# Softmax row sums taken from the value matmuls, through two columns of ones behind each head's values

## The chip, the cores and the metric

The kernel runs on one core of one Trainium2 chip. The number compared is device time in microseconds for one launch, a median over runs. The core has five engines with queues of their own: TensorE (PE in the profile, with its weight loads as PEld), VectorE (DVE), ScalarE (ACT), GpSimd (POOL) and SyncE (SP, which only issues DMAs here). They wait for one another through semaphores alone.

## The reference, cut to what matters

The input `x` is (8, 512, 128). It is normalised, a small chunked attention gives `s`, and a six-layer local-attention transformer gives `g`; the output is `x + s * silu(...)`. The change lies in the attention of the six layers (16 heads of 64, windows of 32 positions, each looking at itself and the window before):

```python
def attn_layer(x, Wqkv, qs, ksc, Wo):
    q, k, v = jnp.split(x @ Wqkv, 3, -1)          # each (b, 512, 1024), 16 heads of 64
    q, k = rotary(l2norm(q) * qs), rotary(l2norm(k) * ksc)
    bk2, bv2 = look(k), look(v)                   # the window before and the window itself
    sim = einsum('bhwie,bhwje->bhwij', q, bk2) * 8, masked
    attn = softmax(sim, -1)                       # over 64 keys
    return einsum('bhwij,bhwje->bhwie', attn, bv2) @ Wo
...
for i in range(6):
    x = attn_layer(shift_tokens(x), ...) + x
    x = ffn_layer(shift_tokens(x), ...) + x       # layer norm, W1, gelu gate, W2
```

The kernel divides by the softmax denominator after the product with the values, not before: `out = (exp(sim - max) @ v) / rowsum(exp(sim - max))`.

## The kernel before

After the setup and the chunked attention (the first 0.7 ms) the program runs six layers. In a layer each of the eight sequences is one **round** (`round_`), so there are 48 rounds; a last, partial one drains the pipeline. A round has eight **iterations** `i = 0..7`, one for each pair of heads, and every engine runs its own loop over `i`, written out by hand. Nothing reorders the work: the order on an engine is the order in the code, and the semaphores (`cur["ssq"]`, `cur["o"]`, ...) tie the engines together. Iteration `i` mixes stages of different pairs: projection and norms of pair `i`, scores of pair `i - 1`, values and outputs of pair `i - 3` (modulo 8, across rounds).

What stands in one iteration, by engine, in order:

- **PE**: `project(i, 0)` (q: six matmuls L782 to L784), `middle` (chunks of v, or feed-forward matmuls of the sequence), `values(i)` (L857), `project(i, 1)` (k), `turn_probs` (L832, transposes of the probabilities), `squares(i, 0)` (L798, L799: sums of squares for the norm of q), `scores` (L812 mask, L822), `turn_out` (L870), `squares(i, 1)` (the same for k), `end`.
- **DVE**: `rotary(i, 0)` (`rb` L1090 and `ra` L1092 read PSUM; `sqlo` L1094 reads two operands in SBUF), `outputs(i)` (L1120 writes `on`), `rotary(i, 1)`, `guard(i, 0)` (L1101), `row_sums(i)` (L1129 sums the rows of `pr`, L1132 takes the reciprocal), `guard(i, 1)` (L1101), `subtract_max(i)` (L1108, L1111). In iteration 4 the DVE also does `fc` (L1162) behind `outputs` and `fl` (L1168) between `guard(4, 0)` and `row_sums`; in 6 two feed-forward products `gx` (L1140) ahead of `outputs`.
- **ACT**: `square` (L960), `exp` (L993), `values_read` (L975: a chunk of v from PSUM to the tile `v`), `inverse_norm` (L966, L968), `pt` (L1014), `oT` (L1028).
- **POOL**: `normalise(i, 1)` (L1054 on `kn`), `rotate` (L1047, the additions `qn` and then `kn`), `normalise(i, 0)` (L1054 on `qn`). All read two operands in SBUF.
- **SP**: twice a round, two DMAs (L1071, L1072) that copy half of `v` shifted by one window into its second plane.

`guard(i, k)` waits for `ssq`, which `squares(i, k)` on PE signals; PE's `squares(i, 1)` in turn waits for `guard(i, 0)`, since both use the bank `SS`. `rb` of `rotary(i, k)` waits for `project(i, k)`.

The value matmuls of `values(i)`: for each of 8 windows in two row groups and 2 heads, 32 matmuls of 64 rows by 32 columns of weights (`pt`) over 64 columns of `v`. The profile counts 64 for them, two for each matmul in float32, and as many for the scores. They wait for `pt`, for the last `outputs`, in iterations 3 and 7 for the DMAs of `v`, and in iterations 4, 5, 6 their second half waits for a reader of the bank (`filled`).

Of the kernel before, what the change touches and what calls it, by code (L numbers as in the profile page):

```python
# [20 lines left out]
P = 128  # L21
# [18 lines left out]
INNER = HEADS * DH  # L40
HP = HEADS // 2
HALF = DH // 2
DI = int(D * 4 * 2 / 3)
NJ = -(-DI // P)
JW = [min(P, DI - P * j) for j in range(NJ)]
# [472 lines left out]
def transformer(nc, t, ctx, sb0, sem, clear, con, ident, ps, xT, d_raw, d_ff):  # L518
# [5 lines left out]
    def sb(name, shape, dt=F32):  # L524
# [20 lines left out]
    pairr = sb("pairr", [P, P], F32R)  # L545
    pairb = sb("pairb", [P, P], BF16)
    xhs, xls = sb("xhs", [P, 2, S], F32R), sb("xls", [P, 2, S], F32R)
    v = sb("v", [P, 2, TB, INNER])
    sq = sb("sq", [P, 2, S])
    sqlo = sb("sqlo", [P, 2, S], F32R)  # L550
    r1 = sb("r1", [P, 2, S])
# [24 lines left out]

    names = ("xh v vev ab sq sl rot g ssq r ln add qkn S m sub exp rs ri pt ptev o oev ot otev wo x1 "
             "fx mean fc fq var fe fr fn fh fl w1 gx gl h w2 x2 shifted cleared").split()  # L580
    sets = [{n: sem(f"r{k}_{n}") for n in names} for k in range(2)]
    A, BB, SS, S0, S1, TT, O0, O1 = range(8)
# [15 lines left out]
    with nc.Block(no_gpsimd_drain=True) as block:  # L598
        @block.sync
        def _(sp):  # L600
            sp.dma_start(raw[:], t["L0_ffn_Wqkv"][0]).then_inc(d_raw, 16)
            for i, n in ((0, "L0_ffn_q_scale"), (2, "L0_ffn_k_scale")):
                src = t[n].rearrange("l (d o) -> d l o", o=1)
                for g in range(4):
                    own, other = (g % 2) * HALF, (1 - g % 2) * HALF
                    sp.dma_start(svec[g * HALF:(g + 1) * HALF, :, i:i + 1], src[own:own + HALF],
                                 allow_slow_non_contiguous=True).then_inc(d_w, 16)
                    sp.dma_start(svec[g * HALF:(g + 1) * HALF, :, i + 1:i + 2],
                                 src[other:other + HALF], allow_slow_non_contiguous=True).then_inc(d_w, 16)
            sp.wait_ge(d_w, 16 * 16)  # L610

        @block.scalar
        def _(act):
            act.wait_ge(s_vz, 1)
            for i, n in ((V_G, "L0_ffn_ln_g"), (V_B, "L0_ffn_ln_b"), (V_B2, "L0_ffn_b2")):
                act.dma_start(vecs[:, :, i:i + 1], t[n].rearrange("l (d o) -> d l o", o=1),
                              allow_slow_non_contiguous=True).then_inc(d_vec, 16)
            b1 = t["L0_ffn_b1"].rearrange("l (d o) -> d l o", o=1)
            for a in range(2):
                for j in range(NJ):  # L620
                    o = a * DI + j * P
                    c = V_B1 + a * NJ + j
                    act.dma_start(vecs[0:JW[j], :, c:c + 1], b1[o:o + JW[j]],
                                  allow_slow_non_contiguous=True).then_inc(d_vec, 16)
            act.wait_ge(d_vec, 16 * (3 + 2 * NJ))

        @block.gpsimd
        def _(pool):

            zeros = (wo[:], w2[:], vec[:], v[:, 1], qn[:], kn[:], pt[:])  # L630
            for z in zeros:
                nc.gpsimd.memset(z, 0.0).then_inc(s_set, 1)
            for z in (w1h, w1l, xhs, xls):
                nc.gpsimd.memset(z[:].bitcast(F32), 0.0).then_inc(s_set, 1)
            for z in (pr, r1, stat):
                nc.gpsimd.memset(z[:], 1.0).then_inc(s_set, 1)
            pool.wait_ge(s_set, len(zeros) + 7)

        @block.vector
        def _(dve):  # L640
            nc.vector.memset(vecs[:], 0.0).then_inc(s_vz, 1)
            nc.vector.memset(v[:, 0], 0.0).then_inc(s_vz, 1)
            nc.vector.memset(oT[:], 0.0).then_inc(s_vz, 1)
            nc.vector.memset(fx[:], 0.0).then_inc(s_hi, 1)
            nc.vector.memset(gx[:], 0.0).then_inc(s_hi, 1)
            nc.vector.memset(xT[:, B, :], 0.0).then_inc(s_hi, 1)
            nc.vector.tensor_copy(maskb[:], con[:, C_MASK:C_MASK + 256]).then_inc(s_hi, 1)
            nc.vector.tensor_copy(identb[:], ident).then_inc(s_hi, 1)
            nc.vector.tensor_copy(pairr[:], con[:, C_PAIR:C_PAIR + P]).then_inc(s_hi, 1)
            nc.vector.tensor_copy(pairb[:], con[:, C_PAIR:C_PAIR + P]).then_inc(s_hi, 1)  # L650
            dve.wait_ge(s_hi, 7)
            dve.wait_ge(s_vz, 3)
# [88 lines left out]
    def round_(k, follows, half, pb, nb, drain=False):  # L741
# [6 lines left out]
        def live(i, lag):  # L748
            return full or i < lag
# [28 lines left out]
        def tensor(pe):  # L778
# [57 lines left out]
            def values(i):  # L836
# [9 lines left out]
                for whi in range(2):  # L846
# [3 lines left out]
                    for tb in range(TB):  # L850
                        for wlo in range(2):
                            for e in range(2):
                                strip = (tb % 2 * 2 + wlo) * WIN
                                c = (e * 2 + tb // 2) * P + strip
                                o = (tb // 2) * P + e * DH
                                hh = 2 * hp + e
                                last = nc.tensor.matmul(  # L857
                                    ps[strip:strip + WIN, O0 + whi, o:o + DH],
                                    pt[whi * DH:(whi + 1) * DH, (i - 1) % 2, c:c + WIN],
                                    v[whi * DH:(whi + 1) * DH, 1 - wlo, tb, hh * DH:(hh + 1) * DH],  # L860
                                    start=True, stop=True, skip_group_check=True,
                                    tile_position=(whi * DH, strip))
                last.then_inc(cur["o"], 1)
# [89 lines left out]
        def scalar(act):  # L953
# [16 lines left out]
            def values_read(j):  # L970
# [1 line left out]
                if j == 4:  # L972
                    act.wait_ge(cur["o"], 3)
                hf, tb = j // 4, j % 4
                nc.scalar.copy(v[:, 0, tb, hf * 512:(hf + 1) * 512], ps[:, V_AT[j][2], :]).then_inc(cur["vev"], 1)  # L975

            def gate(j, bank, n):

# [85 lines left out]
        def sync(sp):  # L1064

            for hf in range(2 if full else 0):
                c = slice(512 * hf, 512 * hf + 512)
                sp.wait_ge(cur["vev"], 4 * hf + 4)
                if hf:
                    sp.wait_ge(cur["o"], 3)  # L1070
# [13 lines left out]
        def vector(dve):  # L1084
# [30 lines left out]
            def outputs(i):  # L1115

                dve.wait_ge(cur["o"], i + 1)
                after(dve, "ri", i)
                after(dve, "ot", i)
                nc.vector.tensor_tensor(  # L1120
                    on[:].rearrange("p (w g d) -> p w g d", w=2, g=4),
                    ps[:, O0:O1 + 1, 0:256].rearrange("p w (g d) -> p w g d", g=4),
                    stat[:, (i - 1) % 2, 2, :].rearrange("p (w g) -> p w g", w=2).unsqueeze(3)
                    .broadcast_to([P, 2, 4, DH]), ALU.mult).then_inc(cur["oev"], 1)

            def row_sums(i):
                b = i % 2
                dve.wait_ge(cur["exp"], i + 1)
                nc.vector.tensor_reduce(stat[:, b, 1, :], pr[:, b, :].rearrange("p (g k) -> p g k", g=8),  # L1129
                                        AX_X, ALU.add).then_inc(cur["rs"], 1)  # L1130
                dve.wait_ge(cur["rs"], i + 1)
                nc.vector.reciprocal(  # L1132
                    stat[:, b, 2, :].rearrange("p (w t e) -> p e t w", w=2, t=2),
                    stat[:, b, 1, :].rearrange("p (e t w) -> p e t w", e=2, t=2)).then_inc(cur["ri"], 1)

            def gated(j, bank, n):
                m = JW[j]
# [6 lines left out]
            for i in range(HP):  # L1144
# [21 lines left out]
                if i == 4:  # L1166
                    dve.wait_ge(cur["fh"], 1)
                    nc.vector.tensor_tensor(fl[:], fc[:], fh[:].bitcast(F32), ALU.subtract).then_inc(cur["fl"], 1)  # L1168
                if live(i, 2):
                    row_sums(i)  # L1170
                if full:
                    guard(i, 1)
                if i == 6:
# [106 lines left out]
```

## Time and profile before

| | before |
|---|---|
| median of 3 runs | 5195.39 us (5191.45 to 5198.09) |
| span of the profiled execution | 5196.3 us |
| PE busy | 4059.5 us (78%) |
| DVE busy | 4157.5 us (80%) |
| ACT busy | 2852.2 us (55%) |
| POOL busy | 2552.5 us (49%) |

The span is from the first to the last instruction of one profiled execution, and it lies inside the range of the timed runs, so what is around it is too small to be seen. The busy shares are means over stages that differ: the first 0.7 ms have little PE work. A high share does not say that an engine is waited for. In the timeline each row is one instruction, or a few alike in a row (x2, x64), with its start and its length in us; what stands in brackets is how long its engine had been idle before it and who ended the wait. On DVE a row begins about 0.08 us before the one ahead of it ends when nothing holds it, so starts 0.60 apart belong to lengths of 0.68.

### The profile page before, as it was taken

What the parts mean: (1) busy time and instruction counts of PE and PEld (TensorE: products, weight loads), DVE (VectorE), ACT (ScalarE), POOL (GpSimd) and SP (SyncE); (2) the same over time, 40 slices, a digit from 0 to 9 for tenths busy, and PEclk for the clock granted to TensorE, in tenths of its full rate; (3) what the DMA queues carried; (4) which work ended last, traced back from release to release, by engine and by line L of the source; (5) the groups of instructions that cost most, each with busy time, mean ns of one, the idle gap of its engine ahead of it and who ended that gap; (6) DMA issues with size and microseconds to landing.
All of it is one profiled execution on the core that took longest, in us unless ns stands there. A gap on an engine that the chain in (4) does not pass through costs nothing. (4 is left out here: it accounts for less than half of the span.)

```text
span 5196.3 us, 147973 instructions
## 1 busy us (share of the span) xinstructions
PE 4059.5 (78%) x62298; PEld 2893.8 (56%) x63066; DVE 4157.5 (80%) x6032; ACT 2852.2 (55%) x4736; POOL 2552.5 (49%) x1604
## 2 busy tenths in 40 slices
PE   2012048999979999789999789999799997899996
PEld 2011036666656666566666566666566665666664
DVE  5977978888878888778888788888788887788885
ACT  1011036666656666556666566666566665565665
POOL 3665844544435544445455445445355444454542
PEclk8566579999989999999999999999899999999998
DMA  0000011111111111111111111111111111111112
GB/s 21 0 6 6 0 43 37 25 25 25 25 45 25 25 25 25 33 37 25 25 25 25 33 37 25 25 25 25 46 25 25 25 25 33 37 25 25 25 25 57
DMA packets 86314, 139.19 MB, mean 27 GB/s; under 512 B 14457, under 2 KB 35600, under 8 KB 83984
## 3 DMA queue, kind: packets, MB, share of 16 engines
q1 hardware_dynamic: 78698, 127.06, 9.3%
q8 instruction: 524, 8.59, 0.7%
q10 hardware_dynamic: 6950, 2.39, 0.2%
q14 instruction: 142, 1.16, 0.1%
HBM read 30.59 MB, written 4.46 MB: 7 GB/s over the span
## 5 line engine op out<-in xcount | busy, mean ns | idle before, releaser
L1054 POOL TENSOR_TENSOR kn<-kn,r 128x512 f32<-128x512 f32 x385 | 495.6, 1287 | 1659.0 <-ACT r L968 1659.0
L960 ACT ACTIVATE sq<-ps 128x512 f32<-128x512 f32 x768 | 459.3, 598 | 905.8 <-PE ps L784 901.7
L1090 DVE TENSOR_TENSOR rb<-ps,tab 128x512 f32<-128x512 f32 x768 | 527.7, 687 | 404.7 <-PE ps L784 346.1
L966 ACT ACTIVATE r<-r 128x512 f32<-128x512 f32 x769 | 485.7, 632 | 567.3 <-DVE r L1101 566.7
L1054 POOL TENSOR_TENSOR qn<-qn,r 128x512 f32<-128x512 f32 x384 | 495.4, 1290 | 550.0 <-ACT r L968 550.0
L1047 POOL TENSOR_TENSOR kn<-ra,rb 128x512 f32<-128x512 f32 x384 | 631.2, 1644 | 79.7 <-DVE ra L1092 70.2
L1094 DVE TENSOR_TENSOR sqlo<-sq 128x512 fp32r<-128x512 f32 x768 | 644.9, 840 | 0.0
L782 PE MATMUL ps<-xhs,wl 128*128 128x512 f32 x768 | 403.5, 525 | 237.3 <-PEq L122 178.5
L1101 DVE TENSOR_SCALAR r<-ps 128x512 f32<-128x512 f32 x768 | 524.2, 683 | 29.0 <-remote 10.5
L1047 POOL TENSOR_TENSOR qn<-ra,rb 128x512 f32<-128x512 f32 x384 | 537.6, 1400 | 0.0
L857 PEld LDWEIGHTS ps<-v,pt 64*32 64x32 f32 x24768 | 394.2, 108 | 243.7 <-issue 186.9
L1092 DVE TENSOR_TENSOR ra<-ps,tab 128x512 f32<-128x512 f32 x768 | 522.2, 680 | 5.7 <-ACT sq L960 5.7
L857 PE MATMUL ps<-v,pt 64*32 64x64 f32 x24768 | 472.6, 223 | 44.7 <-DVE gx L1140 34.1
L968 ACT ACTIVATE r<-r 128x512 f32<-128x512 f32 x769 | 485.5, 631 | 24.4
L798 PE MATMUL ps<-sqlo,pairr 128*128 128x512 f32 x768 | 364.3, 474 | 146.0 <-DVE r L1101 146.0
L822 PE MATMUL ps<-kn,qn 64*32 64x64 f32 x24640 | 426.2, 220 | 19.0 <-POOL kn L1054 15.9
L822 PEld LDWEIGHTS ps<-kn,qn 64*32 64x32 f32 x24640 | 364.0, 106 | 105.2 <-POOL kn L1054 70.1
L418 PE MATMUL ps<-con,ob 128*128 128x128 f32 x36 | 9.9, 431 | 521.3 <-DVE ob L510 521.3
L1120 DVE TENSOR_TENSOR on<-ps,stt 128x512 f32<-128x512 f32 x387 | 265.9, 687 | 105.3 <-PE ps L857 105.3
L913 PE MATMUL ps<-oT,wo 128*128 128x512 f32 x784 | 346.6, 595 | 3.8
L782 PEld LDWEIGHTS ps<-xhs,wl 128*128 128x128 f32 x768 | 146.7, 191 | 312.5 <-issue 244.2
L782 PE MATMUL ps<-xhs,sl 128*128 128x512 f32 x768 | 309.2, 403 | 0.0
(182 smaller groups left out, 9161.1 us busy)
## 6 DMA issues: line engine op xcount, KB each, us to landing
v<-v SPq DMA_DIRECT2D x96, 768.0 KB, 5.8
v<-v SPq DMA_DIRECT2D x96, 192.0 KB, 5.7
raw<-in_L_ffn_Wqkv SPq DMA_DIRECT2D x7, 1536.0 KB, 7.3
tab<-in_rotary SPq DMA_DIRECT2D x6, 1024.0 KB, 5.7
raw<-in_L_ffn_Wo SPq DMA_DIRECT2D x6, 512.0 KB
sT<-so ACTq DMA_DIRECT2D x3, 768.0 KB, 3.3
xnat<-in_L_attn_hidden_states SPq DMA_DIRECT2D x8, 256.0 KB, 3.4
srow<-sT SPq DMA_DIRECT2D x8, 256.0 KB, 3.1
```

The lines of the kernel that those rows point to most:

```text
L782: nc.tensor.matmul(dst, al, bh, start=True, stop=False)
L822: last = nc.tensor.matmul(ps[strip:strip + WIN, S0 + e, col:col + 2 * WIN], q[:, wd * WIN:(wd + 1) * WIN], k[:, wd * WIN:(wd + 2) * WIN], ...
L857: last = nc.tensor.matmul(ps[strip:strip + WIN, O0 + whi, o:o + DH], pt[whi * DH:(whi + 1) * DH, (i - 1) % 2, c:c + WIN], v[whi * DH:(whi ...
L960: nc.scalar.activation(sq[:, k, :], ps[:, A, :], ACT.Square).then_inc(cur["sq"], 1)
L966: nc.scalar.activation(r1[:, k, :], r1[:, k, :], ACT.Ln, scale=RN * RN).then_inc(cur["ln"], 1)
L968: nc.scalar.activation(r1[:, k, :], r1[:, k, :], ACT.Exp, scale=-0.5).then_inc(cur["r"], 1)
L1047: nc.gpsimd.tensor_tensor(dst, ra[:, k, :], rb[:, k, :], ALU.add).then_inc(cur["add"], 1)
L1054: nc.gpsimd.tensor_tensor(dst, dst, r1[:, k, :], ALU.mult).then_inc(cur["qkn"], 1)
L1090: nc.vector.tensor_tensor(rb[:, k, :], ps[:, BB, :], tab[:, 2 * k + 1, :], ALU.mult)
L1092: nc.vector.tensor_tensor(ra[:, k, :], ps[:, A, :], tab[:, 2 * k, :], ALU.mult).then_inc(cur["rot"], 1)
L1094: nc.vector.tensor_tensor(sqlo[:, k, :], sq[:, k, :], sq[:, k, :].bitcast(BF16)[:, 1::2], ALU.subtract).then_inc(cur["sl"], 1)
L1101: nc.vector.tensor_scalar(r1[:, k, :], ps[:, SS, :], 1e-24, None, ALU.max).then_inc(cur["g"], 1)
```

## The change

`v` gets 66 columns a head (`DV = DH + 2`) in place of 64; the two behind the values hold ones from the setup on, in both planes. `values` runs over 66 columns, so that columns 64 and 65 of each head's result are the row sum of the same probabilities; a head's result takes 66 columns of PSUM in place of 64. `row_sums` is gone. `outputs` waits for `o`, takes the reciprocal of column 64 of each of the eight results straight from PSUM, waits for it, and multiplies. `values_read` copies a chunk in eight pieces of 64 columns with a step of 66. The DMAs of `v` carry 528 columns a row in place of 512.

```diff
+DV = DH + 2
-    v = sb("v", [P, 2, TB, INNER])
+    v = sb("v", [P, 2, TB, HEADS * DV])
-            zeros = (wo[:], w2[:], vec[:], v[:, 1], qn[:], kn[:], pt[:])
+            zeros = (wo[:], w2[:], vec[:], qn[:], kn[:])
...
-            for z in (pr, r1, stat):
-                nc.gpsimd.memset(z[:], 1.0).then_inc(s_set, 1)
+            for z in (pr[:], r1[:], stat[:], v[:, 1], pt[:]):
+                nc.gpsimd.memset(z, 1.0).then_inc(s_set, 1)
...
-            nc.vector.memset(v[:, 0], 0.0).then_inc(s_vz, 1)
+            nc.vector.memset(v[:, 0], 1.0).then_inc(s_vz, 1)
...  values(i)
-                                o = (tb // 2) * P + e * DH
+                                o = (tb // 2 * 2 + e) * DV
                                 hh = 2 * hp + e
                                 last = nc.tensor.matmul(
-                                    ps[strip:strip + WIN, O0 + whi, o:o + DH],
+                                    ps[strip:strip + WIN, O0 + whi, o:o + DV],
                                     pt[whi * DH:(whi + 1) * DH, (i - 1) % 2, c:c + WIN],
-                                    v[whi * DH:(whi + 1) * DH, 1 - wlo, tb, hh * DH:(hh + 1) * DH],
+                                    v[whi * DH:(whi + 1) * DH, 1 - wlo, tb, hh * DV:(hh + 1) * DV],
...  values_read(j)
-                nc.scalar.copy(v[:, 0, tb, hf * 512:(hf + 1) * 512], ps[:, V_AT[j][2], :]).then_inc(cur["vev"], 1)
+                nc.scalar.copy(v[:, 0, tb, hf * 8 * DV:(hf + 1) * 8 * DV].rearrange("p (h d) -> p h d", h=8)[:, :, 0:DH],
+                               ps[:, V_AT[j][2], :].rearrange("p (h d) -> p h d", h=8)).then_inc(cur["vev"], 1)
...  sync
-                c = slice(512 * hf, 512 * hf + 512)
+                c = slice(8 * DV * hf, 8 * DV * (hf + 1))
...  outputs(i)
                 dve.wait_ge(cur["o"], i + 1)
-                after(dve, "ri", i)
+                o4 = ps[:, O0:O1 + 1, 0:4 * DV].rearrange("p w (g d) -> p w g d", g=4)
+                ri = stat[:, (i - 1) % 2, 2, :].rearrange("p (w g) -> p w g", w=2).unsqueeze(3)
+                nc.vector.reciprocal(ri, o4[:, :, :, DH:DH + 1]).then_inc(cur["ri"], 1)
+                dve.wait_ge(cur["ri"], i + 1)
                 after(dve, "ot", i)
                 nc.vector.tensor_tensor(
-                    on[:].rearrange("p (w g d) -> p w g d", w=2, g=4),
-                    ps[:, O0:O1 + 1, 0:256].rearrange("p w (g d) -> p w g d", g=4),
-                    stat[:, (i - 1) % 2, 2, :].rearrange("p (w g) -> p w g", w=2).unsqueeze(3)
+                    on[:].rearrange("p (w g d) -> p w g d", w=2, g=4), o4[:, :, :, 0:DH], ri
                     .broadcast_to([P, 2, 4, DH]), ALU.mult).then_inc(cur["oev"], 1)
-            def row_sums(i):
...
                 if i == 4:
                     dve.wait_ge(cur["fh"], 1)
                     nc.vector.tensor_tensor(fl[:], fc[:], fh[:].bitcast(F32), ALU.subtract).then_inc(cur["fl"], 1)
-                if live(i, 2):
-                    row_sums(i)
                 if full:
                     guard(i, 1)
```

Where instructions stand now, first on DVE in iteration 2, from `outputs` to `subtract_max` (`r` is the tile `r1` of the two guards, `stt` the tile of maxima, sums and reciprocals); before:

```order
L1120 TENSOR_TENSOR on<-ps,stt 128x512
L1090 TENSOR_TENSOR rb<-ps,tab 128x512
L1092 TENSOR_TENSOR ra<-ps,tab 128x512
L1094 TENSOR_TENSOR sqlo<-sq 128x512
L1101 TENSOR_SCALAR r<-ps 128x512
L1129 TENSOR_REDUCE stt<-pr 128x8
L1132 RECIPROCAL stt<-stt 128x2x2x2
L1101 TENSOR_SCALAR r<-ps 128x512
L1108 TENSOR_REDUCE stt<-ps 128x8
L1111 TENSOR_TENSOR pr<-ps,stt 128x512
```

and after:

```order
L1122 RECIPROCAL stt<-ps 128x8
L1125 TENSOR_TENSOR on<-ps,stt 128x512
L1092 TENSOR_TENSOR rb<-ps,tab 128x512
L1094 TENSOR_TENSOR ra<-ps,tab 128x512
L1096 TENSOR_TENSOR sqlo<-sq 128x512
L1103 TENSOR_SCALAR r<-ps 128x512 x2
L1110 TENSOR_REDUCE stt<-ps 128x8
L1113 TENSOR_TENSOR pr<-ps,stt 128x512
```

The sum over `pr` has gone from between the two guards, which now follow each other directly, and the reciprocal has moved up, to right ahead of `on`, where it reads PSUM.

On PE in iteration 2, from the last matmuls of `project(2, 0)` over `values(2)` to `project(2, 1)`; before:

```order
L783 MATMUL ps<-xls,sh 128x512
L784 MATMUL ps<-xhs,sh 128x512
L782 MATMUL ps<-wh,xls 128x512
L783 MATMUL ps<-wl,xhs 128x512
L784 MATMUL ps<-wh,xhs 128x512
L857 MATMUL ps<-v,pt 32x64 x32
L782 MATMUL ps<-xhs,wl 128x512
```

and after:

```order
L784 MATMUL ps<-xls,sh 128x512
L785 MATMUL ps<-xhs,sh 128x512
L783 MATMUL ps<-wh,xls 128x512
L784 MATMUL ps<-wl,xhs 128x512
L785 MATMUL ps<-wh,xhs 128x512
L858 MATMUL ps<-v,pt 32x66 x32
L783 MATMUL ps<-xhs,wl 128x512
```

Nothing moves on PE, nor on ACT, POOL (in the rounds) and SP; the 32 value matmuls of an iteration have 66 columns in place of 64.

## Rows read from the trace of the kernel before

**Rows 1.** The page, part 1: busy us, share of the span, instructions of each engine

```profile
PE 4059.5 (78%) x62298; PEld 2893.8 (56%) x63066; DVE 4157.5 (80%) x6032; ACT 2852.2 (55%) x4736; POOL 2552.5 (49%) x1604
```

**Rows 2.** Timeline (start us, us, engine line op out<-in xcount), iteration 1

```profile
2574.07 1.27 POOL L1047 TENSOR_TENSOR qn<-ra,rb 128x512 f32<-128x512 f32 x1
...
2574.52 1.36 DVE L1094 TENSOR_TENSOR sqlo<-sq 128x512 fp32r<-128x512 f32 x1
...
2575.81 0.68 DVE L1101 TENSOR_SCALAR r<-ps 128x512 f32<-128x512 f32 x1
2576.41 0.67 DVE L1129 TENSOR_REDUCE stt<-pr 128x8 f32<-128x512 f32 x1
...
2576.63 0.47 PE L798 MATMUL ps<-sqlo,pairr 128*128 128x512 f32 x1 [0.67 <-DVE r L1101]
...
2577.11 0.20 DVE L1132 RECIPROCAL stt<-stt 128x8 f32<-128x8 f32 x1
...
2577.38 0.69 DVE L1101 TENSOR_SCALAR r<-ps 128x512 f32<-128x512 f32 x1
```

**Rows 3.** Timeline of iteration 6 of the same round

```profile
2628.78 0.69 PE L857 MATMUL ps<-v,pt 64*32 64x64 f32 x32 [0.71 <-DVE gx L1140]
...
2632.37 0.68 DVE L1094 TENSOR_TENSOR sqlo<-sq 128x512 fp32r<-128x512 f32 x1
2632.39 1.79 POOL L1047 TENSOR_TENSOR qn<-ra,rb 128x512 f32<-128x512 f32 x1
...
2633.94 0.48 PE L798 MATMUL ps<-sqlo,pairr 128*128 128x512 f32 x1
...
2634.70 0.69 DVE L1101 TENSOR_SCALAR r<-ps 128x512 f32<-128x512 f32 x1 [0.21 <-remote]
```

**Rows 4.** Groups by line: x count | busy us, mean ns of one | idle before

```profile
L1101 DVE TENSOR_SCALAR r<-ps 128x512 f32<-128x512 f32 x768 | 524.2, 683 | 29.0 <-remote 10.5
...
L913 PE MATMUL ps<-oT,wo 128*128 128x512 f32 x784 | 346.6, 595 | 3.8
...
L1108 DVE TENSOR_REDUCE stt<-ps 128x8 f32<-128x512 f32 x385 | 261.6, 680 | 2.8 <-PE ps L822 2.8
L1129 DVE TENSOR_REDUCE stt<-pr 128x8 f32<-128x512 f32 x386 | 259.1, 671 | 0.0
...
L1028 ACT COPY oT<-ps 128x512 f32<-128x512 f32 x387 | 219.8, 568 | 7.9 <-PE ps L870 7.9
L975 ACT COPY v<-ps 128x512 f32<-128x512 f32 x384 | 217.3, 580 | 24.0 <-PE ps L784 23.9
...
L1132 DVE RECIPROCAL stt<-stt 128x8 f32<-128x8 f32 x386 | 79.3, 205 | 13.2
```

**Rows 5.** Timeline of iteration 4, into the start of iteration 5

```profile
2612.19 1.16 DVE L1168 TENSOR_TENSOR fl<-fc,fh 128x512 fp32r<-128x512 f32 x1
...
2614.09 0.65 DVE L1101 TENSOR_SCALAR r<-ps 128x512 f32<-128x512 f32 x1
...
2615.42 0.39 PE L784 MATMUL ps<-xhs,sh 128*128 128x512 f32 x1
...
2615.85 0.60 ACT L960 ACTIVATE sq<-ps 128x512 f32<-128x512 f32 x1 [0.70 <-PE ps L784]
...
2615.98 0.68 DVE L1090 TENSOR_TENSOR rb<-ps,tab 128x512 f32<-128x512 f32 x1
```

**Rows 6.** Timeline of DVE in iteration 2: the wait before the second rb

```profile
2582.40 0.69 DVE L1090 TENSOR_TENSOR rb<-ps,tab 128x512 f32<-128x512 f32 x1 [0.62 <-PE ps L784]
```

**Rows 7.** Timeline of PE in iteration 3: the value matmuls and what follows

```profile
2596.14 1.14 PE L857 MATMUL ps<-v,pt 64*32 64x64 f32 x64
...
2597.21 0.50 PE L782 MATMUL ps<-xhs,wl 128*128 128x512 f32 x1
```

**Rows 8.** The page, part 6: DMA issues, KB each, median us to landing

```profile
v<-v SPq DMA_DIRECT2D x96, 768.0 KB, 5.8
```

**Rows 9.** Timeline of SP in the same round: the issue of v's second DMA

```profile
2581.23 0.64 SPq L1072 DMA_DIRECT2D v<-v  x1
```

More of the change, by code:

```diff
@@ L570, in transformer @@
     s_w = sem("s_w")
-    names = ("xh v vev ab sq sl rot g ssq r ln add qkn S m sub exp rs ri pt ptev o oev ot otev wo x1 "
+    names = ("xh v vev ab sq sl rot g ssq r ln add qkn S m sub exp ri pt ptev o oev ot otev wo x1 "
              "fx mean fc fq var fe fr fn fh fl w1 gx gl h w2 x2 shifted cleared").split()
@@ L634, in _ @@
                 nc.gpsimd.memset(z[:].bitcast(F32), 0.0).then_inc(s_set, 1)
-            for z in (pr, r1, stat):
-                nc.gpsimd.memset(z[:], 1.0).then_inc(s_set, 1)
-            pool.wait_ge(s_set, len(zeros) + 7)
+            for z in (pr[:], r1[:], stat[:], v[:, 1], pt[:]):
+                nc.gpsimd.memset(z, 1.0).then_inc(s_set, 1)
+            pool.wait_ge(s_set, len(zeros) + 9)
         @block.vector
@@ L1117, in outputs @@
                 dve.wait_ge(cur["o"], i + 1)
-                after(dve, "ri", i)
+                o4 = ps[:, O0:O1 + 1, 0:4 * DV].rearrange("p w (g d) -> p w g d", g=4)
+                ri = stat[:, (i - 1) % 2, 2, :].rearrange("p (w g) -> p w g", w=2).unsqueeze(3)
+                nc.vector.reciprocal(ri, o4[:, :, :, DH:DH + 1]).then_inc(cur["ri"], 1)
+                dve.wait_ge(cur["ri"], i + 1)
                 after(dve, "ot", i)
                 nc.vector.tensor_tensor(
-                    on[:].rearrange("p (w g d) -> p w g d", w=2, g=4),
-                    ps[:, O0:O1 + 1, 0:256].rearrange("p w (g d) -> p w g d", g=4),
-                    stat[:, (i - 1) % 2, 2, :].rearrange("p (w g) -> p w g", w=2).unsqueeze(3)
+                    on[:].rearrange("p (w g d) -> p w g d", w=2, g=4), o4[:, :, :, 0:DH], ri
                     .broadcast_to([P, 2, 4, DH]), ALU.mult).then_inc(cur["oev"], 1)
-            def row_sums(i):
[L1127 to L1134, printed above, removed]
             def gated(j, bank, n):
```

## The prediction, made before the changed kernel had run

> **What bounds the kernel now.** I first read the busy times, to see what invites the change: DVE is busy for 4157.5 us, 80% of the span, more than any other engine [rows 1], and the change takes work from it. But a share does not show what is waited for, so I went on to the timeline, around the place where the row sums stand, and asked of each DVE instruction whether it starts when DVE is free or when somebody lets it.
>
> Iteration 1 [rows 2]: `guard(1, 0)` (first L1101) ends at 2576.49, PE's `squares(1, 1)` (L798) starts at 2576.63, 0.14 later, since it waits for that guard, and `guard(1, 1)` (second L1101) starts at 2577.38, 0.75 after L798. The row sum (L1129) and its reciprocal (L1132) fill the time between, to 2577.31. So DVE is already idle, for 0.07 us, when `guard(1, 1)` begins. The reader is to see that the row sums stand in the shadow of two matmuls: guard, 0.14, 0.75, guard is a ring between DVE and PE which the sums are not in.
>
> That 0.07 could also be the usual step after a short instruction. Iteration 6 decides it [rows 3]: there L798 starts late, at 2633.94, and `guard(6, 1)` starts at 2634.70, after an idle 0.21; again 0.76 after L798. A quarter of a microsecond more room changes nothing in the distance. Whole trace: L1101 has 29.0 us of idle time before it, 10.5 of them put down to `remote` [rows 4]. That is 48 times the 0.21 of iteration 6; the other 18.5 us over the 288 guards of six iterations a round are 0.064 each, so what iteration 1 shows holds in all rounds. That makes seven of eight iterations.
>
> What then sets the pace in iterations 0, 1, 2 and 5 is POOL: `sqlo` takes 1.36 us at 2574.52 where it takes 0.68 elsewhere, and ends at 2575.88, 0.54 after POOL's addition `qn` (2574.07 to 2575.34) [rows 2, 3]. It starts at PE's word but ends at POOL's, so PE's path has 0.68 to spare in such an iteration. In iterations 3 and 7 `sqlo` takes 0.68 and the path runs through PE. In 4 it runs through ACT and `fl`, in 6 through ACT and POOL.
>
> **The change, part by part.** Row sums removed: 386 × 0.671 = 259 us of DVE work go [rows 4]. On the path that is worth 0 in seven iterations, as shown; late next, at once, is PE's `ssq`. Iteration 4 is the exception: `fl` ends at 2613.35, by when `ssq` has arrived, and `guard(4, 1)` starts only at 2614.09 [rows 5]. It will start at about 2613.27, 0.82 sooner. What follows it is maxima, subtraction, and `rb` of iteration 5 at 2615.98. PE's last matmul for that `rb` ends at 2615.81, and ACT's `sq`, ahead of the exponential, starts at 2615.85 on the same matmul [rows 5]. PE is at work without a break from the end of `fl` on. So DVE gains 0.82 and then waits for PE: 0, or at the very best 48 × 0.82 = 39 us.
>
> Reciprocal moved: it took 0.205 [rows 4], then 0.034 until its reader may start, and `on` loses its 0.08 of overlap: `on` ends 0.32 later. From PSUM it may be dearer: the nearest rows are the two reductions of 512 elements, 0.680 from PSUM and 0.671 from SBUF [rows 4], so 0.01 more. The Trainium skill (VectorE: DVE Perf Modes, § The TRN2 errata) gives PSUM sources 62 cycles more than SBUF sources, which at its 0.96 GHz would be an estimated 0.065 us; the two reductions do not bear that out, and either figure is hidden. Behind `on` DVE waits for `project(i, 1)`; the smallest such wait of the round read is 0.62, in iteration 2 [rows 6], and in iteration 4 `fc` waits for ACT there instead. Cover 0.62 against 0.33: cost 0. Bounds: below 0 nothing, since `on` only gets later; above, if it took as long as a full PSUM reduction, 0.68 + 0.11 = 0.79 against 0.62 leaves 0.17 in iteration 2, which POOL's slack of 0.68 hides as well. PE's `turn_out`, the other reader of `on`, comes only after the scores. In the drain nothing covers it: three iterations × 0.33 = 1.0 us, once.
>
> Two more columns: 64 matmul instructions take 1.07 us, from 2596.14 to the next matmul at 2597.21, 16.7 ns each [rows 7]. If that scales with columns, 1.07 × 2/64 = 0.033 an iteration; if it is bound by issue, 0. If the added columns ran one after another at L913's rate, 346.6 us/(784 × 512) = 0.86 ns a column [rows 4], 64 × 2 × 0.86 = 0.110. I take 0.033, the row's own rate. It is on the path in iterations 3 and 7: 96 × 0.033 = 3.2 us (0 to 10.6); in the others the slack covers it. The Trainium skill (TensorE: Matmul & The Clock Gate, § Back-to-back issue gap) gives N/2.4 + 2.5 ns; 64 to 66 columns would add an estimated 0.053 us an iteration, 5.1 us in the sum. Its 29 ns an instruction are not what the rows show (16.7); its result lies inside the bounds.
>
> ACT's copies of v in pieces of 64: the nearest row is L1028, which already writes strided runs of 32 elements, 0.568, against 0.580 for L975 itself [rows 4]. I take 0, with ±0.012 on the path five times a round (iterations 0, 1, 2 and twice 4): ±2.9 us.
>
> DMAs of v, 3% larger: 5.8 us to landing [rows 8], the second of a pair issued at 2581.23 [rows 9], needed by `values(3)` at 2596.14 [rows 7]. It lands near 2587; even at twice the time it would be 3 us early. The other pair is issued in iteration 5 for iteration 7. Cost 0. The fills in the setup are as many, a few per cent longer: under 0.1 us.
>
> Sum, against the span of 5196.3: 0 + 0 + 1.0 + 3.2 + 0 = +4.2 us. The span is 0.9 above the median of the runs, well inside their scatter, so I carry the sum to the median: 5195.4 + 4.2 = 5199.6 us.
>
> **The rivals.**
>
> *DVE is the bound after all.* Its 80% [rows 1] speak for it: a mean instruction removed would count, 0.671 × 386 = 259 us less, 4936 us. The Trainium skill (VectorE: DVE Perf Modes, § Rules for kernel authors) sides with it: `tensor_reduce` on a hot path is the slowest kind and to be restructured away. Against it are the constant 0.75 and the idle 0.21 of iteration 6. A weaker form is that iteration 4 alone pays: 5195.4 − 39 + 4 = 5160. Together 6%.
>
> *POOL gets ahead of `sqlo` in iteration 6.* There `sqlo` starts at 2632.37 and POOL's `qn` at 2632.39; `sqlo` goes first in 0.68, and `qn` is stretched to 1.79 [rows 3]. In iteration 1, where `qn` came first, `sqlo` had to wait for its end. `sqlo(6, 1)` hangs on the second half of `values(6)` (2628.78), which waits for a product of DVE, so its added columns are not covered; POOL's start hangs on ACT and stays. Half of 0.033 is 0.017, the margin 0.02 plus whatever lateness still counts as in time, which the trace does not tell. If it flips, `sqlo` ends at `qn`'s end + 0.54, 2632.39 + 1.27 + 0.54 = 2634.20 in place of 2633.05. `guard(6, 0)` ends 0.60 behind it, and 0.14 more puts L798 at 2634.94, 1.0 later than 2633.94: 48 × 1.0 = +48 us, 5248 us. It decides as soon as the half's columns cost more than the margin. Against it: the proportional estimate stays under it, and `sqlo` need not start first, only be waiting when POOL's previous instruction lets go. 10%. The Trainium skill (SBUF — State Buffer, § SBUF: two separate sides) calls this an exclusive lock between GpSimd and a VectorE operation with two SBUF inputs, held for the whole instruction; by that rule the step is all or nothing, as rows 2 and 3 show.
>
> *The columns run one after another.* +10.6 + 1.0: 5207 us, or more if offsets of 264 bytes slow the copies or the reads as well. Nothing in the trace has such offsets. 10%.
>
> **How the numbers follow.** The forecast 74%, the flip 10%, serial columns 10%, DVE-bound 6%. No change means within 0.2%, 10.4 us, about what a measurement of this kernel can tell: 5185 to 5205.8. The forecast lies there almost wholly (0.72 of its 0.74, the rest slower by its upper bounds); serial columns and the flip are slower (0.08 of the former, leaving 0.02 same); DVE-bound is faster. Faster 0.06, same 0.74, slower 0.20. The range: below, 5199.6 − 3.2 − 2.9 and the runs' scatter of 4, less a little for iteration 4: 5187. Above, serial columns with dear copies: 5207 + 2.9 + 4 = 5214. Flip and DVE-bound, 16%, stay outside.
>
> **What would show it.** Both guards on DVE 0.9 apart as before, now with some 0.8 of idle time before the second, put down to PE; DVE's busy time lower by about 250 us with the span unchanged; the value matmuls at 1.07 to 1.11 for their 64; the wait before the second `rb` shorter by about 0.3. It is wrong if the second guard comes nearer than 0.75 to L798, if `sqlo` in iteration 6 takes over 1 us, or if the wait before `rb` is gone in iterations 3 and 7.

## The result and the profile after

The changed kernel takes 5222.97 us (median of 4 runs, 5218.69 to 5230.6) against 5195.14 us for the kernel before on the same chip: ratio 1.0051, 95% interval 1.0039 to 1.0063. It is slower, by 28 us, outside the range of 5187 to 5214 us; the forecast was no change.

**Totals first.** The page of the changed kernel, part 1 (busy us, share of the span, instructions):

```profile
span 5228.8 us, 147588 instructions
...
PE 4083.7 (78%) x62298; PEld 2913.3 (56%) x63066; DVE 3951.9 (76%) x5647; ACT 2853.0 (55%) x4736; POOL 2550.9 (49%) x1604
```

Against [rows 1] DVE is busy for 205.6 us less, and the span is 32.5 us longer. The prediction looked for about 250 us less: the lengths of the rows sum to 238 us less, since `sqlo` grew by 15.7, and the busy time counts a stretch in which two rows overlap only once. The groups by line of the same kernel (x count | busy us, mean ns of one | idle before):

```profile
L1096 DVE TENSOR_TENSOR sqlo<-sq 128x512 fp32r<-128x512 f32 x768 | 660.6, 860 | 0.0
...
L1103 DVE TENSOR_SCALAR r<-ps 128x512 f32<-128x512 f32 x768 | 525.9, 685 | 305.7 <-remote 305.7
...
L858 PE MATMUL ps<-v,pt 64*32 64x66 f32 x24768 | 484.3, 225 | 49.4 <-DVE gx L1133 39.6 <-PEq L123 3.5
...
L1122 DVE RECIPROCAL stt<-ps 128x8 f32<-128x8 f32 x387 | 79.2, 205 | 112.7 <-PE ps L858 112.5
```

The guards' idle time went from 29.0 [rows 4] to 305.7 us: most of what the row sums and the reciprocal occupied is now waiting, and the profile puts it down to `remote`, as it did the 0.21 in [rows 3]. The reciprocal costs 205 ns from PSUM, as it did from SBUF. Only `sqlo` grew by more than a few us: 860 ns on average, 840 before.

**Then by iteration.** An iteration is taken from the start of one subtraction of the maxima (L1113) to the start of the next; each column sums the 48 rounds, worked out from the traces. Iteration 0 also holds the layers' boundaries and varies by some us between executions of one kernel, so it stands apart.

```
us, sum of 48     it.0   it.1   it.2   it.3   it.4   it.5   it.6   it.7    1 to 7
before           659.7  460.2  434.3  765.9  561.5  477.3  553.0  478.1    3730.4
after            664.7  459.9  434.5  767.2  523.2  516.0  575.2  479.6    3755.5
```

Iteration 4 is 38.3 us shorter, iteration 5 gives 38.7 back, 3 and 7 are 0.03 us longer per round, and iteration 6 is 22.2 us longer. The last is nearly all of the 25.1 us. It is not spread: 26 rounds take 11.52 us there as before, and 22 take 12.53.

**The two kinds of round.** Iteration 6 in an undisturbed round, timeline of the changed kernel (start us, us, engine, line, op, out<-in; idle before in brackets):

```profile
978.41 0.60 ACT L961 ACTIVATE sq<-ps 128x512 f32<-128x512 f32 x1 [0.82 <-PE ps L785]
...
978.48 0.69 DVE L1092 TENSOR_TENSOR rb<-ps,tab 128x512 f32<-128x512 f32 x1 [0.15 <-PE ps L785]
...
981.09 0.71 PE L858 MATMUL ps<-v,pt 64*32 64x66 f32 x32 [0.69 <-DVE gx L1133]
...
984.70 1.82 POOL L1049 TENSOR_TENSOR qn<-ra,rb 128x512 f32<-128x512 f32 x1
984.70 0.68 DVE L1096 TENSOR_TENSOR sqlo<-sq 128x512 fp32r<-128x512 f32 x1
```

And in the round after it:

```profile
1065.88 0.60 ACT L961 ACTIVATE sq<-ps 128x512 f32<-128x512 f32 x1 [0.82 <-PE ps L785]
...
1066.30 0.69 DVE L1092 TENSOR_TENSOR rb<-ps,tab 128x512 f32<-128x512 f32 x1 [0.50 <-PE ps L785]
...
1068.90 0.71 PE L858 MATMUL ps<-v,pt 64*32 64x66 f32 x32 [1.04 <-DVE gx L1133]
...
1072.16 1.27 POOL L1049 TENSOR_TENSOR qn<-ra,rb 128x512 f32<-128x512 f32 x1
...
1072.51 1.47 DVE L1096 TENSOR_TENSOR sqlo<-sq 128x512 fp32r<-128x512 f32 x1
...
1074.73 0.47 PE L799 MATMUL ps<-sqlo,pairr 128*128 128x512 f32 x1 [0.78 <-DVE r L1103]
```

ACT's `sq` and DVE's `rb` wait for the same signal, that of the last matmul of `project(6, 0)`, and normally start 0.07 apart (978.41 and 978.48). In the second round `rb` starts 0.42 after `sq`, 0.35 late; the profile puts the wait down to PE, but `sq` shows that this signal had come, and no other semaphore came late. DVE's product `gx`, the second half of the values (981.09 - 978.41 = 2.68 after `sq`, then 3.02) and the second `sqlo` (6.29 after `sq`, then 6.63) are 0.34 later. POOL's `qn` hangs on ACT and is not: 6.29 and 6.28 after `sq`. So POOL is first, and `sqlo` ends 0.55 after the addition: it takes 1.47 us instead of 0.68, as in [rows 2]. Such a round is 1.0 us longer.

Of the 22 slow rounds 18 are of this kind, and they are always the same: the loop's body holds two rounds, and these are the second round in each of its 18 passes (three passes in each of six layers). The other 4 are lost by a hair: `sqlo` starts between 1 ns before and 4 ns after `qn`; before, it led by 19 to 40 ns in all 48. These 4 have no late `rb` and are 1.0 us longer too (12.52 to 12.54), so that is the price of POOL's lead by itself; the late start only gives POOL the lead.

**The other views that answer to the rows ahead.** Iteration 1, the ring of guards, of the changed kernel:

```profile
2590.95 0.68 DVE L1103 TENSOR_SCALAR r<-ps 128x512 f32<-128x512 f32 x1
...
2591.77 0.47 PE L799 MATMUL ps<-sqlo,pairr 128*128 128x512 f32 x1 [0.65 <-DVE r L1103]
...
2592.52 0.69 DVE L1103 TENSOR_SCALAR r<-ps 128x512 f32<-128x512 f32 x1 [0.89 <-remote]
```

The second guard starts 0.75 after L799, exactly as in [rows 2], with 0.89 us of idle time where the sums stood. The end of iteration 4, same kernel:

```profile
2627.37 1.15 DVE L1161 TENSOR_TENSOR fl<-fc,fh 128x512 fp32r<-128x512 f32 x1
...
2628.45 0.68 DVE L1103 TENSOR_SCALAR r<-ps 128x512 f32<-128x512 f32 x1
...
2631.03 0.60 ACT L961 ACTIVATE sq<-ps 128x512 f32<-128x512 f32 x1 [0.70 <-PE ps L785]
...
2631.10 0.69 DVE L1092 TENSOR_TENSOR rb<-ps,tab 128x512 f32<-128x512 f32 x1 [0.66 <-PE ps L785]
```

Here the guard starts 1.08 after `fl`, 1.90 in [rows 5]; `rb` of iteration 5 starts 3.73 after `fl`, 3.79 before. DVE has won 0.82 and waits 0.66 of it for PE. Iteration 2's second `rb` and iteration 3's values answer to [rows 6, 7]:

```profile
2597.55 0.69 DVE L1092 TENSOR_TENSOR rb<-ps,tab 128x512 f32<-128x512 f32 x1 [0.38 <-PE ps L785]
...
2611.29 1.17 PE L858 MATMUL ps<-v,pt 64*32 64x66 f32 x64
...
2612.38 0.50 PE L783 MATMUL ps<-xhs,wl 128*128 128x512 f32 x1
```

The wait fell from 0.62 to 0.38 and did not end; 64 value matmuls take 1.09 us to the next matmul, 1.07 before.

### The profile page after: what moved, and what is told of

The parts are those of the page before. It is cut to its first block and busy times, and to the rows that moved or that the text cites. A ratio compares the mean times of both kernels' runs of the same rounds, so it can differ in the third digit from the quotient of the medians.

```text
span 5228.8 us, 147588 instructions
## 1 busy us (share of the span) xinstructions
PE 4083.7 (78%) x62298; PEld 2913.3 (56%) x63066; DVE 3951.9 (76%) x5647; ACT 2853.0 (55%) x4736; POOL 2550.9 (49%) x1604
## 3 DMA queue, kind: packets, MB, share of 16 engines
q14 instruction: 141, 1.16, 0.1%
## 5 line engine op out<-in xcount | busy, mean ns | idle before, releaser
L1103 DVE TENSOR_SCALAR r<-ps 128x512 f32<-128x512 f32 x768 | 525.9, 685 | 305.7 <-remote 305.7
L1096 DVE TENSOR_TENSOR sqlo<-sq 128x512 fp32r<-128x512 f32 x768 | 660.6, 860 | 0.0
L1049 POOL TENSOR_TENSOR qn<-ra,rb 128x512 f32<-128x512 f32 x384 | 526.7, 1372 | 0.0
L858 PE MATMUL ps<-v,pt 64*32 64x66 f32 x24768 | 484.3, 225 | 49.4 <-DVE gx L1133 39.6
L799 PE MATMUL ps<-sqlo,pairr 128*128 128x512 f32 x768 | 364.8, 475 | 158.7 <-DVE r L1103 158.7
L784 PE MATMUL ps<-xls,sh 128*128 128x512 f32 x768 | 309.7, 403 | 0.0
```

Of the source, the lines that this page charges most:

```text
L858: last = nc.tensor.matmul(ps[strip:strip + WIN, O0 + whi, o:o + DV], pt[whi * DH:(whi + 1) * DH, (i - 1) % 2, c:c + WIN], v[whi * DH:(whi ...
L1049: nc.gpsimd.tensor_tensor(dst, ra[:, k, :], rb[:, k, :], ALU.add).then_inc(cur["add"], 1)
L1096: nc.vector.tensor_tensor(sqlo[:, k, :], sq[:, k, :], sq[:, k, :].bitcast(BF16)[:, 1::2], ALU.subtract).then_inc(cur["sl"], 1)
L1103: nc.vector.tensor_scalar(r1[:, k, :], ps[:, SS, :], 1e-24, None, ALU.max).then_inc(cur["g"], 1)
```

## The experiments

Three groups, each on one chip beside runs of the kernel before. That kernel took 5214 us beside the first and the third group and 5196 beside the second. The stage ahead of the rounds takes some 736 us in some profiled executions and some 750 in others, of either kernel, so I compare ratios and the iterations' sums. "Ahead" is the number of rounds of 48 in which `sqlo` of iteration 6 takes over 1 us, that is, in which POOL was ahead.

```
                         ratio (95%)              it.4   it.5   it.6   it.7  1 to 7  ahead
before                                           561.5  477.3  553.0  478.1  3730.4    0
after                    1.0051 (1.0039-1.0063)  523.2  516.0  575.2  479.6  3755.5   22
after, again             1.0056 (1.0042-1.0070)  523.2  516.1  571.3  479.5  3751.9   18
before + columns         1.0008 (0.9999-1.0017)  561.8  477.8  553.0  479.7  3734.7    0
after - columns          1.0032 (1.0020-1.0044)  523.2  516.4  571.2  478.0  3749.6   18
after, code 4 on         1.0021 (1.0011-1.0030)  523.1  516.0  552.6  486.1  3739.5    0
after, code 14 on        1.0008 (0.9999-1.0017)  523.2  516.1  553.5  479.5  3734.1    1
before, code 98 on       1.0060 (1.0046-1.0074)  561.6  477.6  571.8  477.8  3749.2   17
after, POOL waits in 6   1.0017 (1.0008-1.0026)  523.2  516.2  558.4  479.7  3739.9    0
before, sqlo delayed     0.9999 (0.9990-1.0008)  561.9  478.3  552.7  478.3  3732.2    0
after, waits in five     0.9782 (0.9768-0.9795)  523.3  486.8  556.8  479.4  3645.7    0
before, waits in five    0.9773 (0.9759-0.9786)  561.5  447.0  553.0  478.1  3636.0    0
```

(In the last two rows POOL waits in five of the eight iterations.)

Theory A: 18 of the lost rounds come from a place in VectorE's program. The change makes that program shorter, so that the first `rb` of iteration 6 comes to lie at this place, where 0.35 us are enough to put POOL first. The rivals: the columns cause it, or it is chance.

**1. The same code, four instructions further on** (waits that are long met, in the setup):

```diff
+            for _ in range(8):
+                dve.wait_ge(s_vz, 3)
```

> The changed kernel with four more waits on DVE in the setup, each already met, so that all of DVE's code for the rounds lies four instructions further on; nothing else differs. Theory A (the place of the code): in the changed kernel DVE starts rb of iteration 6 0.35 us late in the second round of the loop's body, 18 rounds, at one place of its program, and there POOL gets ahead of sqlo, 1.0 us each. The late start moves to the maxima behind the second guard, where DVE is busy for 0.68 anyway: the 18 lost places are gone, 5223 - 18 = 5205 us, and 0 to 8 of the 48 rounds are left in which sqlo of iteration 6 comes second. Theory B (the 66 columns, or their stride, do it): nothing changes, 5223.

Eight such waits are four instructions of VectorE (the page counts 147592 in place of 147588). All of the loss in iteration 6 is gone (552.6, none ahead), with nothing of the computation changed. The late start itself is not gone, and it is not at the maxima, where I expected it. It moved to the first round of the body, to the second `rb` of iterations 1 and 7; in iteration 1 the slack covers it, in 7 it costs 18 × 0.36 = 6.5 us. Iteration 1 of such a round, timeline:

```profile
924.72 0.60 ACT L963 ACTIVATE sq<-ps 128x512 f32<-128x512 f32 x1 [0.59 <-PE ps L787]
...
925.15 0.69 DVE L1094 TENSOR_TENSOR rb<-ps,tab 128x512 f32<-128x512 f32 x1 [1.01 <-PE ps L787]
```

Again 0.43 after `sq` instead of 0.07.

**2. The columns alone**: the kernel before with the 66-column layout, its row sums and reciprocal kept, the columns' sums not used.

```diff
+DV = DH + 2
-    v = sb("v", [P, 2, TB, INNER])
+    v = sb("v", [P, 2, TB, HEADS * DV])
...
-                                o = (tb // 2) * P + e * DH
+                                o = (tb // 2 * 2 + e) * DV
```

> The kernel before with the 66 columns alone: v, its copies, its DMAs, the value matmuls and the strided read of their results are those of the change; the row sums stay on DVE as before, and the two added columns are read by nobody. DVE's program has the instructions of before at their old places. Theory A: iterations 3 and 7 each 0.03 longer, 2.9 us, and in 0 to 8 rounds POOL gets ahead of sqlo in iteration 6 since its start moves by about 0.025 towards the margin of 0.02: 5198 to 5206. Theory B: all of the loss, 5223.

Iterations 3 and 7 are 1.4 and 1.6 us longer, as in the changed kernel, and iteration 6 loses nothing: `sqlo` leads `qn` by 3 to 28 ns. The columns narrow the lead and by themselves lose no round.

**3. POOL made to wait in iteration 6** until the second `sqlo` is done:

```diff
             n = 2 * i + k
+            if k == 0 and i in (6,):
+                pool.wait_ge(cur["sl"], 2 * i + 2)
```

> The changed kernel, in which POOL waits in iteration 6 for the second sqlo before its addition qn, so that it can't get ahead. Theory A: the lost places of iteration 6 (22 of 48 in the profiled run, 1.0 us each) are gone, 5223 - 22 = 5201 or a little less; POOL's addition loses nothing, since it was blocked by sqlo in the other rounds too. Theory C (what was lost in iteration 6 is a late DVE, and POOL's order does not matter): the 18 late starts of 0.35 stay and cost 6 us, of the rest nothing comes back: 5218 or more.

No `sqlo` is long any more, and 16.8 of the 22.2 us come back. Of the remaining 5.4 over before, 3.7 are late starts: 17 of these rounds take about 11.74, 0.22 more than the others. The other 1.6 are a single late round, of 13.12. In it the granted clock of TensorE was 1.00 from 1257.7 to 1261.5 us, while PE did the same matmuls as in the next late round, and then 0.51 from 1262.0 to 1265.4 us, about the lower of its two levels (1.2 and 2.4 GHz). PE's projection matmuls take 0.63 us there and 0.40 in that next round, which keeps 1.00. So a late start costs 0.22 where POOL waits, and 1.0 where it gives POOL the lead.

**4. `sqlo` of iteration 6 delayed in the kernel before**, by a memset of 8 elements ahead of it:

```diff
+                if (i, k) == (6, 1):
+                    nc.vector.memset(spare[:], 0.0)
```

> The kernel before with one small fill of a spare tile (8 elements) on DVE, in iteration 6 alone, between ra and the second sqlo; nothing reads it. sqlo starts 0.06 to 0.2 us later. Theory A (an exclusive right that goes to whom asks first): POOL is ahead in all 48 rounds, each 1.0 us longer: 5195 + 48 = 5243. Theory C (what is late is late by its own length): at most 0.2 less the 0.14 that PE is behind there, 48 times 0.06 = 3: 5198.

Inconclusive: the memset shifted `sqlo` too little, it still led by 0 to 27 ns, and no round was lost. It shows only that a lead near 0 can still be enough.

**5. The changed kernel again.**

> The changed kernel once more, unaltered, beside the kernel before and the other experiments of this group. Theory A (the loss sits in iteration 6 because POOL's qn addition gets ahead of sqlo there, in the rounds in which VectorE's first product of the iteration starts about 0.35 us late, and in a few by a hair): sqlo of iteration 6 takes over 1 us in 18 to 24 of the 48 rounds, the second round of the loop's body in each pass among them; sum of iteration 6 over 48 rounds 571 to 577 us against 553; kernel +25 to +33 us (ratio 1.005 to 1.006). Rival (a chance of that one execution, no fixed place): under 10 such rounds or others, and +6 to +12 us (1.001 to 1.002), as for the layout alone.

The same 18 rounds are lost, each with the start of `sqlo` 336 to 363 ns behind that of `qn`, and none by a hair, though the other rounds lie between 8 ns ahead and 7 behind. The 18 are fixed; the 4 of the first execution were not.

**6. The kernel before, its code 98 instructions further on**, so that the first `rb` of iteration 6 in the body's second round becomes VectorE's instruction 977, counted in the order of its program. In the changed kernel it is 849; 977 - 849 = 128.

```diff
+            for _ in range(196):
+                dve.wait_ge(s_vz, 3)
```

> The kernel before with its computation untouched, but with about 98 more waits that are long met in VectorE's program ahead of the loop, so that VectorE's code of iteration 6 in the loop's second round comes to lie where it lies in the changed kernel (modulo 128 instructions). Theory A (the late start belongs to a place in VectorE's code): rb of iteration 6 starts about 0.35 us late in the 18 second rounds, sqlo loses its place to POOL's addition there, sum of iteration 6 becomes 571 us against 553 (+1.0 us each), iteration 4 loses nothing; kernel +18 us beside up to 5 us for the waits themselves, 5230 to 5238 where the kernel before has 5213 to 5215 (ratio 1.003 to 1.0045). Rival (the late start comes from the ones columns or the removed row sums, for instance from when TensorE's results come): iteration 6 stays at 553 +/- 1 us and the kernel within +5 us.

Row sums and layout as before, and iteration 6 is 18.8 us longer. `rb` is late in the same 18 rounds; in 17 of them `sqlo` takes over 1 us; in the other it starts 0.90 behind `qn`. In that round the granted clock is 1.00 from 4953 to 4957 us, while PE does the same matmuls as in the late round ahead of it, and 0.72 from 4957 to 4963 us, partly the lower level; the round ahead keeps 1.00. Timeline, iteration 6 of the kernel before so moved:

```profile
1083.48 0.60 ACT L962 ACTIVATE sq<-ps 128x512 f32<-128x512 f32 x1 [0.82 <-PE ps L786]
...
1083.91 0.69 DVE L1092 TENSOR_TENSOR rb<-ps,tab 128x512 f32<-128x512 f32 x1 [0.50 <-PE ps L786]
...
1089.78 1.27 POOL L1049 TENSOR_TENSOR qn<-ra,rb 128x512 f32<-128x512 f32 x1
...
1090.10 1.50 DVE L1096 TENSOR_TENSOR sqlo<-sq 128x512 fp32r<-128x512 f32 x1
```

The changed kernel's loss has been made in the kernel before without a part of the change. The kernel as a whole lost more than expected (ratio 1.006, not 1.003 to 1.0045); the added waits and a long first stage (756.5 us in the profiled execution) are in that, and I did not separate them.

**7 and 8. POOL waits for the second `sqlo` in iterations 0, 1, 2, 5 and 6**, in the changed kernel and in the one before:

```diff
             n = 2 * i + k
+            if k == 0 and i in (0, 1, 2, 5, 6):
+                pool.wait_ge(cur["sl"], 2 * i + 2)
```

> The changed kernel, with POOL's first addition waiting for the second sqlo in iterations 0, 1, 2, 5 and 6 (in all of these sqlo takes over 1 us in many or all rounds, in iteration 6 in 22). Theory A (the lock between POOL's addition and sqlo costs the round about 0.6 to 1.0 us wherever POOL is first): iterations 1, 2 and 5 get 0.5 to 1.0 us shorter each, iteration 6 returns to 11.52, sums -72 to -144 us for 1, 2 and 5 and -22 us for 6, some -20 us for 0; kernel 5060 to 5130 us where the kernel before has 5214 (ratio 0.97 to 0.985). Rival (POOL's chain of addition and normalisation is what the round waits for, so that its later start costs as much as the faster sqlo gives): sums of 1, 2 and 5 unchanged or longer, kernel 5210 to 5250.

> The kernel before with the same waits of POOL in iterations 0, 1, 2, 5 and 6, no ones columns. It tells what the ones columns are worth once POOL's lead is fixed. If the row sums' place on VectorE then lies on the path (theory B), this one is slower than the changed kernel with the same waits by 0.2 us or more in the iterations 1, 2 and 5, 30 us and more in all. If they lie in VectorE's idle time there too (theory A), it is faster than that by the 6 to 10 us which the layout alone costs (0.03 us each in iterations 3 and 7, some 4 at the layers' starts). Where the rival of the run before holds (POOL's chain is the bound), both stand near 5210 to 5250.

Both beat both kernels by over 2%: 5082.94 and 5077.69 us, 5195.68 for the kernel before beside them. Iterations 1, 2 and 5 of the changed kernel get shorter by 31.7, 30.6 and 29.2 us, 0.61 to 0.66 a round. Its iteration 1, timeline:

```profile
2528.32 0.68 DVE L1098 TENSOR_TENSOR sqlo<-sq 128x512 fp32r<-128x512 f32 x1
2528.92 0.68 DVE L1105 TENSOR_SCALAR r<-ps 128x512 f32<-128x512 f32 x1
2529.08 1.27 POOL L1051 TENSOR_TENSOR qn<-ra,rb 128x512 f32<-128x512 f32 x1 [1.20 <-DVE sqlo L1098]
...
2529.74 0.47 PE L799 MATMUL ps<-sqlo,pairr 128*128 128x512 f32 x1
```

`sqlo` takes 0.68, and POOL's addition, now 0.76 behind the start of `sqlo` instead of 0.48 ahead of it, delays nobody. This bears out the prediction's reading that POOL set the pace in these iterations: nearly all of the 0.68 that it gave PE to spare came back. And it answers what the change is worth with POOL out of the way: no gain. Iterations 1 to 7 take 3645.7 us with it, 3636.0 without. 38.2 us gained in iteration 4 are again lost in 5, by 39.8; 3.8 of the rest is the late start (18 × 0.21).

**9. The changed kernel, 14 instructions further on**, with no first product of an iteration at the place.

```diff
+            for _ in range(28):
+                dve.wait_ge(s_vz, 3)
```

> The changed kernel with its computation untouched and 14 more instructions of met waits in VectorE's setup, so that the place at which VectorE started late falls in front of no first product of an iteration, in either round of the loop's body. Theory A (iteration 6's loss and the moved stall of the first shift are both this place): no rb starts late, sqlo of iteration 6 over 1 us in 0 to 5 rounds, sums 553 to 557 for iteration 6, 479.6 for iteration 7, 460 for iteration 1, 516 for iteration 5; kernel +6 to +12 us over before (ratio 1.001 to 1.0025), that is 18 us under the changed kernel. Rival (something of the late start is the change's own): 18 rounds of some iteration still 0.36 us or more longer, +13 us or more (over 1.0025).

No `rb` is late, one round is lost by a hair, and iterations 1 to 7 are 3.7 us over before. Iteration 6 of the body's second round, timeline:

```profile
1064.56 0.60 ACT L963 ACTIVATE sq<-ps 128x512 f32<-128x512 f32 x1 [0.82 <-PE ps L787]
...
1064.63 0.69 DVE L1094 TENSOR_TENSOR rb<-ps,tab 128x512 f32<-128x512 f32 x1 [0.15 <-PE ps L787]
...
1070.85 0.68 DVE L1098 TENSOR_TENSOR sqlo<-sq 128x512 fp32r<-128x512 f32 x1
1070.85 1.81 POOL L1051 TENSOR_TENSOR qn<-ra,rb 128x512 f32<-128x512 f32 x1
```

Its time cannot be told from the kernel before (1.0008, 0.9999 to 1.0017), a little under the 1.001 to 1.0025 expected.

**10. The changed kernel without the columns**: 64 columns a head, and the reciprocal, at its new place, reads a constant 1, so the softmax is not normalised.

```diff
-DV = DH + 2
+DV = DH
...
-                nc.vector.reciprocal(ri, o4[:, :, :, DH:DH + 1]).then_inc(cur["ri"], 1)
+                nc.vector.reciprocal(ri, rs).then_inc(cur["ri"], 1)
```

> The changed kernel without the ones columns: values and their layout as before (64 columns a head), the row sums simply not computed (the reciprocal, in its new place, reads a constant 1, so the softmax is not normalised). VectorE's program is as long as in the changed kernel. Theory A (the loss comes from the shorter program of VectorE, not from the columns): iteration 4 523, iteration 5 516 (gain given back although no column was added), iterations 3 and 7 as before (766, 478), rb of iteration 6 late in the same 18 rounds and sqlo over 1 us in them, sum of iteration 6 571; kernel +16 to +24 us, ratio 1.003 to 1.0045. Rival 1 (the columns cause iteration 6's loss): iteration 6 stays at 553, kernel within 5 us of before. Rival 2 (the columns are what gives iteration 4's gain back): iteration 5 stays at 477 and the kernel is 20 us or more faster than theory A has it.

All three parts came as theory A has them. 38.3 us of iteration 4 are given back by 39.1 in iteration 5 with no column added; 3 and 7 are as before; the same 18 rounds are lost. Timeline, iteration 6:

```profile
1076.87 0.60 ACT L961 ACTIVATE sq<-ps 128x512 f32<-128x512 f32 x1 [0.81 <-PE ps L785]
...
1077.29 0.69 DVE L1092 TENSOR_TENSOR rb<-ps,tab 128x512 f32<-128x512 f32 x1 [0.50 <-PE ps L785]
...
1083.16 1.28 POOL L1049 TENSOR_TENSOR qn<-ra,rb 128x512 f32<-128x512 f32 x1
...
1083.49 1.50 DVE L1096 TENSOR_TENSOR sqlo<-sq 128x512 fp32r<-128x512 f32 x1
```

Both rivals fall. Taking the row sums away, with the reciprocal moved, already makes the kernel slower.

## Why the prediction was wrong

*DVE's removed work is worth nothing in seven iterations*: right. The guard stays 0.75 behind L799, iterations 1 and 2 keep their times, and 7 and 8 show it with POOL held back too.

*Iteration 4's gain is lost again in iteration 5*: right, and the first of the two ends (0, not 39 us). It is shown alone in 10.

*The reciprocal, the copies of v and the DMAs cost nothing*: right. 205 ns from PSUM; the copies' group (L976) has 582 ns for 580; the 792 KB take 5.9 us to landing for 5.8 [rows 8]. The wait that was to fall by about 0.3 fell by 0.24.

*Two columns, 0.033 in iterations 3 and 7, 3.2 us*: right, 0.03 and 2.9 us (1.4 and 1.6 in experiment 2). The line "one after another" (10.6) is out.

*POOL gets ahead of `sqlo` in iteration 6*: this rival came true, and taking it as 10% and as all or nothing is where the prediction failed. Its place and price were right: 1.0 us a round. Its condition was not. I let it hang on the half's columns against a lead of 0.02 us, as one comparison for all 48 rounds. The columns were sized rightly (0.017; they took 12 to 16 ns of the lead in experiment 2) and cost 0 to 4 rounds. What took 18 was not in the sum at all: the length of VectorE's program. Each removed instruction moves all that follow it, and an `rb` that comes to lie at certain places of that program starts 0.35 us late. In the kernel before, no `rb` lay at such a place; in the changed one the first `rb` of iteration 6 does, from which the second half of the values follows by `gx`, the very link that [rows 3] show. An edit that takes instructions from an engine was priced by their durations and by their waits, and not by where the rest of the code comes to lie.

The sum with that term: iterations 3 and 7 +2.9, 18 lost rounds +18, 0 to 4 by a hair, iterations 4 and 5 +0.4, together 21 to 25 us. The two executions of the changed kernel have 21.5 and 25.1 in iterations 1 to 7. The rest of the 28 us lies in iteration 0 and the first stage, which differ by as much between executions of one kernel.

What the place is stays open. Counted as above, the two late `rb` of experiment 1 are instructions 593 and 721, so all four places found lie in steps of 128. The step alone makes nothing late: in the changed kernel 593 and 721 are guards, of iterations 1 and 7, and both follow the row ahead of them as in the other rounds (the second 0.60 after the start of `sqlo` in all 48).

The profile has a DMA queue that carries instructions, in packets of 8 KB. In the changed kernel one of them starts 3.86 to 3.90 us after each of the 18 late `rb`, as here (queues, stretch 1070.1 to 1070.4 us; packets, MB, share):

```profile
q14 instruction: 1, 0.01, 16.1%
```

In 6 and 10 the same packet follows each of the late `rb`, by 3.80 to 3.85 us, in 1 by 0.64 to 0.92. In 9 it comes 1.16 us after the first `rb` of iteration 5, and in the kernel before some 0.5 us after the second `rb` of iteration 4; there nothing is late. This packet starts after the late `rb` and at no fixed distance, so it is not itself what `rb` waited for. The late start moves with the count of VectorE's instructions; that their loading causes it is a guess that was not tried. The Trainium skill (Runtime: NRT & Kernel Launch, § Instruction fetch mechanics) says that an engine fetches its program in blocks by its own queue and that a crossing is mostly hidden; the traces show packets on such a queue, and no run here shows whether the 0.35 us are a crossing that is not hidden.

## What to carry to other kernels

Before you price work taken off an engine, ask for each instruction whether its end or somebody's word lets the next one start; here 259 us of work stood in a wait and were worth nothing. Where two engines share a lock and one leads by 20 ns, give that order a chance of its own and fix it by a wait: an order that no wait had set cost the kernel before 118 us. A changed number of instructions moves the code behind it; if a loss falls on the same rounds of the loop each time and no semaphore explains it, shift the code by a few idle instructions before blaming the edit.

## What was not expected of the hardware

- An `rb` at certain places of VectorE's program (849; 977; 593 and 721) starts 0.35 us late in every pass of the loop, 18 of 18 rounds, in seven traces. Four idle instructions more in the setup move this to other `rb` (experiment 1), 98 bring it into a kernel that had none (experiment 6), and 14 leave none (experiment 9).
- The order of `sqlo` and `qn` at equal starts is not settled by the starts: rounds were lost with `sqlo` 1 ns ahead and kept with it 9 ns behind (experiment 1). The lead also differed between runs of the same computation: by the medians of the rounds with no late `rb`, `sqlo` was 2 ns ahead in experiment 5 and 18 ns ahead in experiment 9. These were on two chips and with the code shifted in one, and which of the two did it is not shown. The Trainium skill (SBUF — State Buffer, § SBUF: two separate sides) has an exclusive lock there that goes to who starts first; rows a third of a microsecond apart agree, and those within some 10 ns do not show who was first.
